# A two-layer relational graph network: layer 2 takes its first relation before its root matrix, and x is loaded into the sums

## What is computed

```python
def _rgcn_conv(x, src, dst, etype, W, root, b):
    x_src = x[src]
    seg = dst * num_rel + etype
    sums = segment_sum(x_src, seg, num_segments=num_nodes * num_rel)
    cnt = segment_sum(ones, seg, num_segments=num_nodes * num_rel)
    mean = (sums / maximum(cnt, 1.0)[:, None]).reshape(num_nodes, num_rel, -1)
    return einsum('nri,rio->no', mean, W) + x @ root + b

h = relu(_rgcn_conv(x, src, dst, edge_type, W1, root1, b1))
out = _rgcn_conv(h, src, dst, edge_type, W2, root2, b2)
return _layernorm(x + out)          # over the 768 features
```

## Time and profile before

| | us |
|---|---|
| median of 3 runs (1611.38 to 1623.99) | 1616.69 |
| the profiled execution | 1620.82 |
| its span in the trace | 1619.0 |
| PE busy / DVE / ACT / POOL | 1515.5 / 1135.7 / 672.4 / 685.6 |
| mean granted TensorE clock | 0.977 of full speed |

### The profile page before, as it was taken

How to read it: one execution, slowest core, us unless ns; L and a number is a source line. 1 busy time by engine, 2 the same in 40 slices (tenths; PEclk the granted TensorE clock), 3 DMA queues, 4 the chain that set the end, 5 groups by cost and what they waited for, 6 DMA issues and landing times.

```text
span 1619.0 us, 24359 instructions
## 1 busy us (share of the span) xinstructions
PE 1515.5 (94%) x9003; PEld 1486.9 (92%) x9003; DVE 1135.7 (70%) x1735; ACT 672.4 (42%) x935; POOL 685.6 (42%) x515
## 2 busy tenths in 40 slices
PE   5999998989999999999897998999999999899996
PEld 5999998988999898899886998999999999899996
DVE  6879999926989567888892211656565656588696
ACT  3222233313556444685461021435444444357541
POOL 1111111214687455866540013636363636477460
PEclk9999999999999999999998999999999999999998
DMA  5353221233676566776552134656565656567552
GB/s 166 114 184 123 83 70 33 69 128 103 185 215 188 189 194 195 227 214 188 169 149 112 39 120 156 192 163 200 159 209 163 205 160 219 161 194 243 161 148 95
DMA packets 109223, 254.42 MB, mean 157 GB/s; under 512 B 18376, under 2 KB 81527, under 8 KB 109063
## 3 DMA queue, kind: packets, MB, share of 16 engines
q0 software_dynamic: 38400, 136.49, 28.6%
q1 hardware_dynamic: 70726, 116.65, 21.3%
HBM read 243.77 MB, written 65.45 MB: 191 GB/s over the span
## 4 chain that ended last, share of the span: by engine, by line
PE 62%; DVE 20%; DMA 10%; issue 4%; POOL 2%; ACT 1%; SPq 0%; ACTq 0%; POOLq 0%; DVEq 0%
PE prod L672 50%; PE agg L700 11%; DMA raw<-y,bucket_index 5%; DVE g_low L925 4%; DVE keyed L1113 3%; DVE slot_hot L1117 3%; DMA y<-y_stage 3%; DVE g_high L925 3%; DMA x_rows<-in_x 2%; POOL raw L432 2%; DVE acc L932 2%; DVE dst_hot L1108 1%; DVE one_hot L919 1%; ACT g_high L527 1%; DVE acc L911 1%
## 5 line engine op out<-in xcount | busy, mean ns | idle before, releaser
L432 POOL DMA_INDIRECT raw<-y,bucket_index x480 | 613.5, 1278 | 471.9 <-DVE g_low L925 256.1
L672 PE MATMUL prod<-w_high,h_high 128*128 128x384 f32 x2160 | 735.9, 341 | 24.1 <-DVE acc L908 11.7
L672 PE MATMUL prod<-w_low,h_high 128*128 128x384 f32 x2160 | 729.8, 338 | 0.0
L672 PE MATMUL prod<-w_high,h_low 128*128 128x384 f32 x2160 | 728.8, 337 | 0.0
L527 ACT ACTIVATE g_high<-raw 128x768 fp32r<-128x768 f32 x480 | 378.1, 840 | 209.7 <-PE agg L700 133.1
L925 DVE TENSOR_TENSOR g_low<-raw,g_high 128x768 fp32r<-128x768 f32 x320 | 293.8, 953 | 231.5 <-ACT g_high L527 231.0
L672 PEld LDWEIGHTS prod<-w_high,h_high 128*128 128x128 f32 x2160 | 411.5, 191 | 26.8 <-issue 21.0
L672 PEld LDWEIGHTS prod<-w_low,h_high 128*128 128x128 f32 x2160 | 411.3, 190 | 0.0
L672 PEld LDWEIGHTS prod<-w_high,h_low 128*128 128x128 f32 x2160 | 410.5, 190 | 0.0
L560 ACT ACTIVATE y_stage<-prod 128x384 f32<-128x384 f32 x280 | 137.5, 491 | 617.5 <-PE prod L672 586.8
L700 PE MATMUL agg<-g_high,one_hot 128*128 128x384 f32 x960 | 252.5, 344 | 34.2 <-DVE g_low L925 28.4
(11 more groups left out here) (109 smaller groups left out, 642.1 us busy)
## 6 DMA issues: line engine op xcount, KB each, us to landing
y<-y_stage SPq DMA_DIRECT2D x280, 187.5 KB
w_raw<-in_w_all SPq DMA_DIRECT2D x36, 1152.0 KB, 7.8
raw<-y,bucket_index POOLq DMA_INDIRECT x480, 5.2
x_rows<-in_x SPq DMA_DIRECT2D x20, 375.0 KB
y<-in_x SPq DMA_DIRECT2D x1, 3750.0 KB, 14.9
y<-acc SPq DMA_DIRECT2D x10, 375.0 KB
out<-acc SPq DMA_DIRECT2D x10, 375.0 KB
bias<-in_b SPq DMA_DIRECT2D x2, 384.0 KB, 11.0
```

The source lines that it names most:

```text
L432: pool.indirect_dma_start(raw[:, slot_of, :], None, y[0:written * N, :], bass.IndirectOffsetOnAxis(ap=bucket_index[:, r * RT + i:r * RT + ...
L672: mm = pe.matmul(prod[:, bank, 0:HALF], left[:, k, t * P:(t + 1) * P], right[:, h, k, :], start=(k == 0 and left is h_high and right is w_ ...
```

## The change

1. Matrix 9 is now relation 1 of layer 2, and matrix 10 is root2 (ROOT2 = R + 2; the loads of the weights are swapped to match). The loop behind them is as it was.
2. x is no longer loaded into x_rows. When h is stored and turned, SP loads the ten tiles of x straight into acc, two loads behind each of the y stores 3 to 7 of relation 1. POOL adds b2 to acc when all ten have landed, and DVE keeps the root's products with an addition (plus="acc"). DVE's ten additions of x are gone.
3. PE waits for all 20 keeps of the root before the loop.
4. In layer 1's root matrix sum_flags stands behind step 1 instead of step 3.

```diff
@@ sync @@
+                m = {ROOT2: ROOT2 - 1, ROOT2 - 1: ROOT2}.get(q, q) if isinstance(q, int) else q
...
+            for s in range(STEPS):
+                store_y(R - 1, 1, s)
+                if s == 3:
+                    sp.wait_ge(transposed, 6 * T)
+                    sp.wait_ge(h_stored, 16 * T)
+                if 3 <= s < 3 + T // 2:
+                    for t in (2 * (s - 3), 2 * (s - 3) + 1):
+                        sp.dma_start(acc[0:ROWS[t], t, :], x[t * NT:t * NT + ROWS[t], :])\
+                            .then_inc(residual_loaded, 16)
+                if s == 8:
+                    load_unit(ROOT2, 0)
+                if s == 14:
+                    load_unit(ROOT2, 1)
             load_unit(ROOT2 + 1, 0)
             load_unit(ROOT2 + 1, 1)
-            sp.wait_ge(transposed, 4 * T)
-            for t in range(T):
-                if t >= 2:
-                    sp.wait_ge(residual_added, t - 1)
-                sp.dma_start(x_rows[0:ROWS[t], t % 2, :],
-                             x[t * NT:t * NT + ROWS[t], :]).then_inc(residual_loaded[t % 2], 16)
-                for s in (2 * t, 2 * t + 1):
-                    store_y(R - 1, 1, s)
...
@@ gpsimd @@
+            pool.wait_ge(residual_loaded, 16 * T)
+            pool.wait_ge(bias_loaded, 32)
             for t in range(T):
-                pool.wait_ge(residual_loaded[t % 2], 16 * (t // 2 + 1))
-                pool.wait_ge(bias_loaded, 32)
-                pool.tensor_tensor(x_rows[:, t % 2, :], x_rows[:, t % 2, :], bias[:, 1, :], ALU.add)\
-                    .then_inc(x_biased, 1)
+                pool.tensor_tensor(acc[:, t, :], acc[:, t, :], bias[:, 1, :], ALU.add).then_inc(x_biased, 1)
@@ scalar @@
-            matrix(ROOT2, None, None, last_turn)
-            matrix(ROOT2 + 1, R - 1, banks(2))
+            matrix(ROOT2 - 1, R - 1, banks(2), last_turn)
+            matrix(ROOT2, None, None)
@@ tensor @@
-                if s == 3:
+                if s == 1:
                     sum_flags()
...
-            matrix(ROOT2, banks(2), kept(2 * STEPS, (root_kept, 2 * STEPS), 2), last_turn)
-            matrix(ROOT2 + 1, banks(2), lambda s: [(root_kept, 3 * STEPS - BANKS + s + 1)] if s < BANKS
-                   else staged(R - 1)(s))
+            matrix(ROOT2 - 1, banks(2), lambda s: kept(2 * STEPS, (root_kept, 2 * STEPS), 2)(s) if s < BANKS
+                   else staged(R - 1)(s) + ([(h_low_ready, 2 * T * 2 + 2 * s + 2)] if s < T else []), last_turn)
+            matrix(ROOT2, banks(2), lambda s: [(y_staged, STEPS * R - BANKS + s + 1) if s < BANKS
+                                               else (root_kept, 2 * STEPS + s - BANKS + 1)])
+            pe.wait_ge(root_kept, 3 * STEPS)
@@ vector @@
+            matrix(ROOT2 - 1, last_turn)
             for s in range(STEPS):
-                if s == 0:
-                    low_of_turn(2, T - 1)
-                    dve.wait_ge(transposed, 6 * T)
-                    dve.wait_ge(h_stored, 16 * T)
-                keep(STEPS * ROOT2 + s, s % T, s // T, banks(2)(s), plus=None)
+                dve.wait_ge(x_biased, s % T + 1)
+                keep(STEPS * ROOT2 + s, s % T, s // T, banks(2)(s), plus="acc")
...
-            for t in range(T):
-                dve.wait_ge(x_biased, t + 1)
-                dve.tensor_tensor(acc[:, t, :], acc[:, t, :], x_rows[:, t % 2, :], ALU.add)\
-                    .then_inc(residual_added, 1)
```

More of the change, by code:

```diff
@@ L74, in rgcn_residual_layernorm @@
     MEAN1 = R
-    ROOT2 = R + 1
+    ROOT2 = R + 2
     MEAN2 = Q - 1
@@ L209, in rgcn_residual_layernorm @@
         bucket_added = sem("bucket_added")
-        residual_loaded = [sem(f"residual_loaded{s}") for s in range(2)]
+        residual_loaded = sem("residual_loaded")
         x_biased = sem("x_biased")
-        residual_added = sem("residual_added")
         var_ready = sem("var_ready")
@@ L300, in load_unit @@
                     sp.wait_ge(w_low_ready, u)
-                w = w_all[bass.ds(q, 1), :, h * HALF:(h + 1) * HALF].rearrange("o (k p) n -> p (o k) n", p=P)
+                m = {ROOT2: ROOT2 - 1, ROOT2 - 1: ROOT2}.get(q, q) if isinstance(q, int) else q
+                w = w_all[bass.ds(m, 1), :, h * HALF:(h + 1) * HALF].rearrange("o (k p) n -> p (o k) n", p=P)
                 sp.dma_start(w_raw[:], w).then_inc(w_loaded, 16)
@@ L357, in _ @@
                 relation(q, q - 1, q)
-            load_unit(ROOT2, 0)
-            load_unit(ROOT2, 1)
+            load_unit(ROOT2 - 1, 0)
+            load_unit(ROOT2 - 1, 1)
             for t in range(T):
@@ L362, in _ @@
                 sp.dma_start(y[t * NT:t * NT + ROWS[t], :], acc[0:ROWS[t], t, :]).then_inc(h_stored, 16)
+            for s in range(STEPS):
[11 more added lines that the diff above has]
+                    load_unit(ROOT2, 1)
             load_unit(ROOT2 + 1, 0)
             load_unit(ROOT2 + 1, 1)
-            sp.wait_ge(transposed, 4 * T)
-            for t in range(T):
-                if t >= 2:
-                    sp.wait_ge(residual_added, t - 1)
-                sp.dma_start(x_rows[0:ROWS[t], t % 2, :],
-                             x[t * NT:t * NT + ROWS[t], :]).then_inc(residual_loaded[t % 2], 16)
-                for s in (2 * t, 2 * t + 1):
-                    store_y(R - 1, 1, s)
[L375 to L378, removed]
             with sp.Fori(2, R) as r:
-                relation(r + ROOT2, stored_before(1, r), r)
+                relation(r + ROOT2 - 1, stored_before(1, r), r)
             for t in range(T):
@@ L645, in _ @@
             matrix(MEAN1, None, None, completing, spilled=(0, R - 1), ahead=True)
-            matrix(ROOT2, None, None, last_turn)
-            matrix(ROOT2 + 1, R - 1, banks(2))
+            matrix(ROOT2 - 1, R - 1, banks(2), last_turn)
+            matrix(ROOT2, None, None)
             with act.Fori(2, R - 1) as r:
-                matrix(r + ROOT2, stored_before(1, r), banks(2), one_relation(r + R - 2, None))
+                matrix(r + ROOT2 - 1, stored_before(1, r), banks(2), one_relation(r + R - 2, None))
             matrix(MEAN2 - 1, 2 * R - 3, banks(2, True), averaging(2 * R - 3, None, 3), ahead=True, high_at=4)
@@ L860, in _ @@
                    spilled=(0, R - 1))
-            matrix(ROOT2, banks(2), kept(2 * STEPS, (root_kept, 2 * STEPS), 2), last_turn)
-            matrix(ROOT2 + 1, banks(2), lambda s: [(root_kept, 3 * STEPS - BANKS + s + 1)] if s < BANKS
-                   else staged(R - 1)(s))
+            matrix(ROOT2 - 1, banks(2), lambda s: kept(2 * STEPS, (root_kept, 2 * STEPS), 2)(s) if s < BANKS
[3 more added lines that the diff above has]
+            pe.wait_ge(root_kept, 3 * STEPS)
             with pe.Fori(2, R - 1) as r:
-                matrix(r + ROOT2, banks(2), staged(stored_before(1, r)), one_relation(r + R - 2, None))
+                matrix(r + ROOT2 - 1, banks(2), staged(stored_before(1, r)), one_relation(r + R - 2, None))
             matrix(MEAN2 - 1, banks(2, True), staged(2 * R - 3, True), averaging(2 * R - 3, None, 3))
@@ L1205, in _ @@
             dve.wait_ge(root_kept, 3 * STEPS)
-            for t in range(T):
-                dve.wait_ge(x_biased, t + 1)
-                dve.tensor_tensor(acc[:, t, :], acc[:, t, :], x_rows[:, t % 2, :], ALU.add)\
-                    .then_inc(residual_added, 1)
[L1210 to L1214, removed]
             with dve.Fori(2, R - 1) as r:
-                matrix(r + ROOT2, one_relation(r + R - 2, r - 1), low_at=((5, 0, K), (12, 0, K)))
+                matrix(r + ROOT2 - 1, one_relation(r + R - 2, r - 1), low_at=((5, 0, K), (12, 0, K)))
             matrix(MEAN2 - 1, averaging(2 * R - 3, R - 2, 3), low_at=in_parts)
```

## The result

| | before | after |
|---|---|---|
| median of 20 runs, us | 1618.92 (1611.38 to 1625.86) | 1614.55 (1611.23 to 1618.53) |
| after / before, 95% interval | | 0.9971 [0.9958, 0.9985] |
| span of the profiled execution | 1619.0 | 1612.9 |
| mean granted TensorE clock | 0.977 | 0.978 |

The account below looks back on a forecast made before the run. TensorE, busy 94%, was taken as the bound, so only its idle or slow-clock time could be won: -32.3 + 1.3 + 0.7 + 24.6 = -5.7 us, from 1616.7 to 1611 us, own range 1605 to 1616, wider range 1597 to 1623.

Parts of the forecast that it names:

- flag sums: Layer 1's root matrix near 350: moving them two steps earlier removes 4.4 us idle and 2.6 us slow clock, -7.0 us.
- wait on acc, first bucket of the loop: Layer 2's start, near 866 and 1004: idle 11.7 and 8.7 us, slow clock 2.2 and 2.7 us, all removed.
- relu behind a staging: ACT at layer 2's start: last relu waits behind a staging, so PE's next transposes come 1.3 us later.
- wait for all keeps of the root: Before layer 2's loop: PE waits until all root steps are kept, +0.7 us.
- loads of x in SP's queue: Relation 1: x loads ahead of y stores on five DMA engines cost 22.4 us waits plus 2.2 slow clock, +24.6.
- The queue laid end to end: SP's transfers from 876 on, in order on five engines: y8 by 919.5, root's weight half by 923.5, step 16 at 926.8.
- DMA share 0.32 from 840 to 915 unbroken: Sign of being right, around relation 1: five of 16 DMA engines carry the transfers throughout, share 0.32.
- The single waits: PE in relation 1, ahead of steps 13 to 16: 3.1, 4.4, 4.4 and 10.5 us, sum 22.4.
- the slow steps between the waits are hidden: Relation 1, steps 13 to 15: slow clock there adds nothing, since the queue sets their pace.
- x stays hidden: First rival, relation 1: PE never waits for the queue, -30.3 us, 1586 us; chance 0.16.
- The clock stays low from step 13 on: Second rival, relation 1: steps 16 to 19 cost 12.5 us extra instead of 2.2; +4.6 us, 1621 us; chance 0.10.
- The flag sums give nothing: Third rival, layer 1: gathers end later waits, so the 7.0 us are lost; +1.3 us, 1618 us; chance 0.12.

## Why the prediction was right

| step | predicted, us | measured |
|---|---|---|
| flag sums | -7.0 | -6.9, -6.9 and -6.6 at the place itself, in three pairs of traces; -6.2 at the turn (-7.3 with the flags alone); -7 to -9 by ratios |
| wait on acc, first bucket of the loop | -25.3 | both gone, bucket and step at full clock |
| relu behind a staging | +1.3 | 1.31 |
| wait for all keeps of the root | +0.7 | 1.14, and 1.13 without x |
| loads of x in SP's queue | +24.6 | 25.3 |
| layer 2's start, net | +1.3 | +2.7 |

**Right, step by step.** The queue laid end to end gave the places: step 16 at 926.8, less 7.0 us for the flag sums 919.8; measured 919.94. That it is this close is partly luck. The store of y3 was seen at 874.64, 1.1 us earlier than laid out (882 + 0.7 - 7.0), and the four pairs of loads with their stores then took 31.07 us instead of 30.0, which made up for it. The loads of x as a whole were off by 0.7 us. Waits of y_stage for the store, of w_high for its load and PE behind both all stand in the rows above. The "DMA share 0.32 from 840 to 915 unbroken" does not: it was broken from 902 to 908 by the weight half. The forecast had given the half a time on the five engines alone; they remained the ones that finished last (917.2 forecast, 917.38 measured). GpSimd's additions took 20.2 us instead of 18.6 from 913.0 on, ended at 933.2, before the first keep at 937.8, and cost nothing, and the gathers began at 939.65, 58 us before the loop, as the prediction let them. Here the Trainium skill's rule from "DMA: Bandwidth & Descriptors", section "Why a DMA increments its semaphore by 16 and not by 1" (a transfer is spread over the largest number of engines, up to 16, that divides its slowest dimension) is borne out with a number: 125 rows 0.33 and 128 rows 0.97 in the same place. Its exception for GpSimd's queue on trn2, where some direct copies use all 16 engines, each with a sixteenth of the rows rounded up, agrees too, with 350 GB/s at 125 rows.

**Right as a sum, wrong in its parts.** The single waits were put at 3.1, 4.4, 4.4 and 10.5 us, 22.4 in all, and the clock at 2.2. Measured are 3.49, 1.66, 4.20 and 8.72, 18.1 in all, and the slow clock holds the other 7.2 of the 25.3: steps 13 to 15 took 6.02, 3.39 and 4.97 us instead of 3.12, and the 24 steps behind the last wait 77.06 instead of 74.9. The step that was mis-sized is "the slow steps between the waits are hidden": they are, but they then *replace* idle time in the sum of waits. After 3.49 us of idleness step 13 ran with its matmuls 0.32 us apart instead of 0.17, was done 2.9 us later, and the next wait shrank from 4.4 to 1.66. Since the queue sets when PE may go on, idle time and slow time together stay the same. The wait for the keeps was priced at 0.7 and was 1.1. Without x the new start gains 22.6 us in the traces (25.3 - 2.7), where the forecast's terms give 23.3 (25.3 - 1.3 - 0.7).

**The rivals.** *x stays hidden* (1586 us): false; PE's four waits for stagings in after are gone in the kernel without x. *The clock stays low from step 13 on* (1621 us): false. 890 to 900 has a mean granted clock of 0.66, as a mix of both levels (1.2 and 2.4 GHz), but step 14 ran at the upper one again, and so did the rest from 924 on. *The flag sums give nothing* (1618 us): false by both pairs. The condition on which the first rival hung, x that does not stand before y, is what the experiments then made true.

**The median.** The prediction stood on the median of three runs of before, 1616.69, and twenty have 1618.92; the measured difference of the medians is 4.4 us where 5.7 were predicted. That the spans differ by 6.1 is no better proof: 2.5 of these lie at places that the change does not touch, and the terms of the change, measured in the same traces, add up to 3.5. So the terms are borne out to about 2 us together, which is also as far as one pair of traces carries.

## What to carry to other kernels

A load that nothing needs soon may still be dear if it shares a queue and a few DMA engines with stores that free buffers: lay the queue end to end, with the engines each transfer really uses, and follow the buffers back to the engine that waits. Look at the DMA share in a stretch of transfers of one kind before moving any; here 0.33 with PE waiting meant that the shape of the transfer, not the amount, was the cost, and another row count or another issuing queue was worth more than the reordering itself (0.9845 and 0.9847, against 0.9971 for the whole change). Before trusting one pair of traces, look where their difference arises: here 2.5 of 6.1 us lay outside the change. Where a queue sets the pace, the idle time and the slow clock behind it are one sum, not two.

## What the runs showed that was not expected

- 125 rows from SP's queue ran at 0.33 and 128 GB/s, 128 rows at 0.97 and 342 GB/s; 125 rows from GpSimd's queue at 0.96 to 1.06 and about 300 to 350 GB/s. The first was read from before, the other two were not.
- The clock behind a wait did not follow the length of that wait alone. In after the first matmul took 0.69 us behind 3.49 and 8.72 us of idleness and 0.44 behind 4.20, where the clock fell only in the course of the step (0.70 from 908 to 912). With the root's weight half first, two waits of the same 2.53 us were followed by 0.44 us (903.86) and by 0.69 us (911.36). What sets it was not tried.
- Additions of 0.96 us on DVE ahead of keeps held PE up for 8.48 us, through the loads that they waited for.
